# Selective scan: the skip term on ScalarE and in accumulating transfers, the norm's place and four engine orders

## What is computed

```
u, z = x @ Win                               # 512 channels each
uc   = silu(convb + sum_k up[k:k+L] * convw[k])          # 4 taps
x_dbl = uc @ Wx;  B, C from it;  dt = softplus(x_dbl @ Wdt + bdt)
h    = exp(dt * A) * h + (dt * uc) * B       # 32 states, scan over tokens
y    = sum_n h[n] * C[n]  +  uc * Dp         # uc * Dp is the skip term
out  = (y * silu(z)) @ Wout, layernorm, then fusion of both directions
```

## Time and profile before

| | us |
|---|---|
| three runs, median | 4105.2 (4103.2 to 4106.7) |
| profiled execution: time, and span of its core | 4104.3, 4102.7 |
| busy: TensorE, VectorE, ScalarE, GpSimd | 3861.7, 3597.1, 2803.0, 2360.9 |

### The profile page before, as it was taken

How to read it: one execution, slowest core, us unless ns; L and a number is a source line. 1 busy time by engine, 2 the same in 40 slices (tenths; PEclk the granted TensorE clock), 3 DMA queues, 4 the chain that set the end, 5 groups by cost and what they waited for, 6 DMA issues and landing times. The chain is left out here.

```text
span 4102.7 us, 69921 instructions
## 1 busy us (share of the span) xinstructions
PE 3861.7 (94%) x19212; PEld 2880.4 (70%) x19213; DVE 3597.1 (88%) x6830; ACT 2803.0 (68%) x4602; POOL 2360.9 (58%) x2013
## 2 busy tenths in 40 slices
PE   6999999999999999999999969999999699999998
PEld 4666666666666666666666637777777588888887
DVE  7999999999999999999999948998998566666665
ACT  5777777777777777777777847777776345444444
POOL 2555545555455554555655566777777455555555
PEclk8898989898888888888988879999999799999999
DMA  2221222222222212222112222222222455555555
GB/s 73 46 49 35 53 45 51 49 39 49 45 52 47 44 46 43 55 45 50 43 40 55 45 54 78 95 95 91 90 98 80 137 95 94 90 102 95 85 94 86
DMA packets 198462, 272.58 MB, mean 66 GB/s; under 512 B 23377, under 2 KB 143058, under 8 KB 198354
## 3 DMA queue, kind: packets, MB, share of 16 engines
q0 software_dynamic: 94432, 130.60, 17.8%
q1 hardware_dynamic: 100480, 138.48, 12.0%
q10 hardware_dynamic: 3442, 2.21, 0.2%
HBM read 121.07 MB, written 150.14 MB: 66 GB/s over the span
## 5 line engine op out<-in xcount | busy, mean ns | idle before, releaser
L618 PE MATMUL pj<-xt,win 128*128 128x512 f32 x3144 | 934.7, 458 | 49.4 <-DVE xt L793 27.1
L618 PEld LDWEIGHTS pj<-xt,win 128*128 128x128 f32 x3144 | 684.5, 221 | 275.4 <-issue 53.1
L2011 POOL DMA_INDIRECT out<-e_y,e_to x272 | 473.5, 1741 | 365.7 <-ACT e_y L2117 305.3
L806 DVE SCALAR_TENSOR_TENSOR uc<-pj,convw,uc 128x511 f32<-128x511 f32 (+2 forms) x780 | 516.8, 728 | 5.4 <-ACT uc L411 5.4
L326 POOL TENSOR_TENSOR wk<-v,uc 128x512 f32<-128x512 f32 x260 | 347.5, 1336 | 281.2 <-DVE v L854 280.4
L301 POOL TENSOR_TENSOR r<-r,neg_half 128x4 f32<-128x4 f32 x64 | 76.1, 1189 | 667.1 <-ACT r L387 667.1
L666 PE MATMUL po<-yz,wout 128*128 128x512 f32 x1024 | 456.6, 599 | 0.0
L2062 PE MATMUL e_p<-e_w,e_a 128*128 128x256 f32 x3264 | 416.0, 284 | 0.7 <-DVE e_a L2172 0.7
L2062 PEld LDWEIGHTS e_p<-e_w,e_a 128*128 128x128 f32 x3264 | 393.7, 188 | 10.8 <-DVE e_a L2172 1.7
L2050 PE MATMUL e_p<-e_xt,e_w 128*128 128x512 f32 x1632 | 395.5, 398 | 4.5 <-DVE e_xt L2164 2.4
L666 PEld LDWEIGHTS po<-yz,wout 128*128 128x128 f32 x1024 | 189.3, 190 | 262.9 <-issue 262.9
(11 more groups left out here) (243 smaller groups left out, 8806.4 us busy)
## 6 DMA issues: line engine op xcount, KB each, us to landing
e_x<-expert_in SPq DMA_DIRECT2D x138, 260.0 KB, 2.6
bb<-bc SPq DMA_DIRECT2D x65, 512.0 KB, 6.0
h_rows<-fb POOLq DMA_DIRECT2D x64, 512.0 KB, 7.2
h_rows<-h0c SPq DMA_DIRECT2D x32, 512.0 KB, 6.0
a_h<-h_rows SPq DMA_DIRECT2D x128, 128.0 KB
out<-a_bs SPq DMA_DIRECT2D x128, 128.0 KB
bc<-xd SPq DMA_DIRECT2D x65, 128.0 KB, 2.3
e_w1s<-in_moe_w POOLq DMA_DIRECT2D x9, 512.0 KB, 5.2
```

Of the source, the lines that this page charges most:

```text
L618: i = mm(pj[m][:], win[d][wp][:, k, c:c + P], xt[xp][:, k, :], start=(k == 0 and n == 0), stop=(k == KD - 1 and n == 2))
L806: stt(uc[d][:, m, to], pj[m][:, of], convw[d][:, m, tap:tap + 1], uc[d][:, m, to], ALU.mult, ALU.add).then_inc(S["cv"], 1)
L2011: pool.indirect_dma_start(out=out, out_offset=bass.IndirectOffsetOnAxis(ap=to[n][:, j:j + 1].bitcast(U32), axis=0), in_=y[n][:, j, :], in_ ...
```

## The change

- The four skip instructions leave VectorE. ScalarE scales `uc` by `Dp` in place (`skip`), and GpSimd issues two accumulating transfers a slot, from `uc` to `qq` within the on-chip memory (`add_input`); `sums` waits for these (`mix0`, `mix1`). The two instructions that stay in `dead_part` read `wk` (= dt * uc) in place of `v`.
- The norm moves up by one slot: `ln_stats(s+2)` on VectorE behind `gate` of the odd slot, `ln_scale(s+2)` on GpSimd behind `gather(s+2)` of the odd slot, `ln_apply(s+2)` on ScalarE ahead of `decays` of the odd slot.
- GpSimd: all four `wk` first, then all four `tp`, then `add_input`; `row_scale` comes behind `keep_residual` or behind `gather` and `ln_scale`.
- ScalarE: `project_copies` moves into `front`, one part after another, with `skip` between.
- TensorE: `x_dbl` in two halves between the halves of z; `fusion` in two halves, on either side of `dt_proj` (and `turn_x`); `dead_sums` between the halves of the next u; `state_sum` between the halves of `out_proj`.

The diff, cut to its core:

```diff
 # GpSimd
+            def scan_inputs(t, d):
+                pool.wait_ge(S["dt_ok"], t + 1)
+                for m in range(MD):
+                    pool.tensor_tensor(wk[:, m, :], v[:, m, :], uc[d][:, m, :], ALU.mult).then_inc(S["dtu_ok"], 1)
                 pool.wait_ge(S["bcast"], 16 * (t + 1))
+                for m in range(MD):
                     pool.wait_ge(S["dtu_ok"], MD * t + m + 1)
...
                     pool.tensor_tensor(tp[:, m, :], wk[:, m, :], bb[d][:, 0, :], ALU.mult).then_inc(S["tp_ok"], 1)
+            def add_input(t, d):
+                for h in range(NP):
+                    mm = slice(2 * h, 2 * h + 2)
+                    wait_apart(pool, S["q_ok"], NP * t + h + 1)
+                    wait_apart(pool, S["du_ok"], MD * t + 2 * h + 2)
...
+                    pool.dma_start(qq[:, mm, :].rearrange("p m n -> p (m n)"),
+                                   uc[d][:, mm, :].rearrange("p m n -> p (m n)"), accum_op=ALU.add
+                                   ).then_inc(S[f"mix{h}"], 16)
             def slots(s, first):
                 for d in range(DIRS):
                     t = 2 * s + d
-                    if d == 0:
-                        ln_scale(s + 1)
+                    add_input(t, d)
                     if not first:
                         add_rows(t - 2, d, s - 1)
+                    if d == 0:
+                        pool.wait_ge(S["hc_ok"], t + 1)
+                        keep_residual(s + 1)
+                    else:
+                        gather(s + 2)
+                        ln_scale(s + 2)
                     if not (first and d == 0):
                         row_scale(t - 1)
...
+                    scan_inputs(t + 1, 1 - d)
 # ScalarE
+            def skip(t, d, tiles):
+                for m in tiles:
+                    act.wait_ge(S["dtu_ok"], MD * t + m + 1)
+                    act.activation(uc[d][:, m, :], uc[d][:, m, :], ACT.Copy, scale=dp[d][:, m:m + 1]
+                                   ).then_inc(S["du_ok"], 1)
+            def front(t, d, copies):
                 uc_silu(t, d, range(2))
+                if copies:
+                    project_copies(t - 2, range(1))
+                    skip(t - 1, 1 - d, range(2))
                 z_silu(t, d, range(2))
                 uc_silu(t, d, range(2, MD))
+                    skip(t - 1, 1 - d, range(2, MD))
+                if copies:
+                    project_copies(t - 2, range(1, KD))
+                z_silu(t, d, range(2, MD))
                 xd_copy(t, d)
...
+            def back(t, d, s_next=None):
+                last_tap_and_bias(t + 1, 1 - d, range(MD))
                 if s_next is not None:
                     ln_apply(s_next)
...
                 decays(t, d)
 # TensorE
                 in_proj(t, d, 1, range(2))
+                x_dbl(t, d, range(2))
+                in_proj(t, d, 1, range(2, MD))
+                x_dbl(t, d, range(2, MD))
                 if back > 1:
-                    fusion(t - 2, d)
+                    fusion(t - 2, d, (0,))
                 dt_proj(t, d)
                 if turn:
                     turn_x(s_next)
+                if back > 1:
+                    fusion(t - 2, d, (1,))
+                    row_squares(t - 2)
...
+                in_proj(t + 1, 1 - d, 0, range(2))
+                dead_sums(t, d)
+                in_proj(t + 1, 1 - d, 0, range(2, MD))
                 dead_count(t)
+                if back > 0:
+                    out_proj(t - 1, 1 - d, range(1))
                 state_sum(t)
                 if back > 0:
+                    out_proj(t - 1, 1 - d, range(1, KD))
 # VectorE
-                    stt(qq[:, mm, :], over_pair(pss[:]), dall[:], v[:, mm, :], ALU.mult, ALU.mult
+                    dve.wait_ge(S["dtu_ok"], MD * t + 2 * h + 2)
+                    stt(qq[:, mm, :], over_pair(pss[:]), dall[:], wk[:, mm, :], ALU.mult, ALU.mult
                         ).then_inc(S["q_ok"], 1)
-                for m in range(MD):
-                    dve.wait_ge(S["q_ok"], NP * t + m // 2 + 1)
-                    stt(qq[:, m, :], qq[:, m, :], dp[d][:, m:m + 1], uc[d][:, m, :], ALU.add, ALU.mult
-                        ).then_inc(S["q2_ok"], 1)
...
-                    if d == 0:
-                        ln_stats(s + 1)
                     dead_part(t, d)
...
                     gate(t, d)
+                    if d == 1:
+                        ln_stats(s + 2)
```

More of the change, by code:

```diff
@@ L145, in mamba_stage @@
           u_ps a_ok z_ps z_ok uc_ok xd_ps xd_ok bc_ok bcast xd_st dt_ps v_ok vc_ok y_ok l_ok w_ok g_ok
-          d0_ok dt_ok dtu_ok tp_ok da_ok h_ok hc_ok q_ok q2_ok yv_ok yz_ok xm_ok qd_ps gt_ok ct_ok cnt_ps
+          d0_ok dt_ok dtu_ok tp_ok da_ok h_ok hc_ok q_ok du_ok mix0 mix1 yv_ok yz_ok xm_ok qd_ps gt_ok ct_ok cnt_ps
           fl_ok s_ps o_ps fo_ok sq_ok ss_ps rv_ok rr_ok f_ps fin_ok h1_st acc gt2 e_bc e_da e_tp e_h e_hc e_y""".split()
@@ L335, in _ @@
             gather(1)
+            ln_scale(1)
             scan_inputs(0, 0)
@@ L476, in decays, with project_copies @@
                     act.activation(y[:, m, :], v[:, m, :], ACT.Exp, scale=amat[d][:, m, 0:1]).then_inc(S["da_ok"], 1)
-            def project_copies(t):
-                for k in range(KD):
+            def skip(t, d, tiles):
[3 more added lines that the diff above has]
+                                   ).then_inc(S["du_ok"], 1)
+            def project_copies(t, parts):
+                for k in parts:
                     act.wait_ge(S["o_ps"], KD * t + k + 1)
@@ L541, in _ @@
             last_tap_and_bias(0, 0, range(MD))
-            front(0, 0)
+            front(0, 0, False)
             scan_weights()
@@ L549, in _ @@
             softplus_log(0)
-            back(0, 0, False)
+            back(0, 0, 1)
             def slots(s, first):
@@ L554, in slots @@
                     t = 2 * s + d
-                    front(t + 1, 1 - d, s + 1 if d == 0 else None)
+                    front(t + 1, 1 - d, not (first and d == 0))
                     more_states(t, d)
@@ L571, in slots @@
                         finish(t - 1, 1 - d)
-                    back(t + 1, 1 - d, True)
+                    back(t + 1, 1 - d, s + 2 if d == 1 else None)
             slots(0, True)
@@ L576, in _ @@
                 slots(s, False)
+            project_copies(2 * NSEQ - 1, range(KD))
             row_var(2 * NSEQ - 1)
@@ L620, in in_proj, with x_dbl @@
                     i.then_inc(S[ps], 1)
-            def x_dbl(t, d):
+            def x_dbl(t, d, tiles):
                 if not (isinstance(t, int) and t == 0):
                     pe.wait_ge(S["fl_ok"], 3 * t)
-                for m in range(MD):
+                for m in tiles:
                     pe.wait_ge(S["uc_ok"], MD * t + m + 1)
                     i = mm(px[0:NXR, :], wx[d][:, m, :], uc[d][:, m, :], start=(m == 0), stop=(m == MD - 1))
-                i.then_inc(S["xd_ps"], 1)
+                if MD - 1 in tiles:
+                    i.then_inc(S["xd_ps"], 1)
             def dt_proj(t, d):
@@ L658, in state_sum, with out_proj @@
                 mm(pss[:], smask0[:], bcp[:], start=True, stop=True).then_inc(S["s_ps"], 1)
-            def out_proj(t, d):
-                for k in range(KD):
+            def out_proj(t, d, parts):
+                for k in parts:
                     if k == 0 and not (isinstance(t, int) and t == 0):
@@ L679, in row_squares, with fusion @@
                 i.then_inc(S["ss_ps"], 1)
-            def fusion(t, d):
+            def fusion(t, d, halves=range(2)):
                 pe.wait_ge(S["fo_ok"], KD * (t + 1))
                 pe.wait_ge(S["sq_ok"], KD * (t + 1))
-                for h in range(2):
+                for h in halves:
                     for jj in range(2):
@@ L941, in _ @@
             out_weights()
+            ln_stats(1)
             dead_test(0, 0)
```

39 lines of the change are left out of this document (8 added, 31 removed).

## The result

The changed kernel takes 4154.8 us (median of 4 runs, 4153.7 to 4164.5) against 4104.9 us (4103.2 to 4106.7) in the runs of the kernel before beside it: a ratio of 1.0127, with a 95% interval of 1.0109 to 1.0144. The forecast was 4175 us, slower. The profiled execution after took 4153.7 us. One of the four runs of experiment 3 came at a lower granted clock (0.80 against 0.92) and took 4394 us; it is left out of that experiment's time.

The account below looks back on a forecast made before the run. VectorE and TensorE were taken as full. The chain's steps summed to 74.9 us a pair against 72.85, times 32 = +66; with a little of rival A, +70 on 4104.3 us: forecast 4175 us, range 4130 to 4230.

Parts of the forecast that it names:

- step 1: Odd slot, from `dt_ok` through GpSimd's products, transfers and gather issue until the gathers have landed: 26.3 us.
- 6 xt_low to dt_ok: Even slot, from `xt_low` to `dt_ok`, all on VectorE as in the kernel before: 13.4 us.
- rival B: Odd slot: gathers land before `gate` ends, at 23.1 us; pair 71.7 us, time 4068 us; chance 0.15.
- upper bound of 30 us: Odd slot: gathers' landing if three large transfers stand ahead in one queue, each moving data for 4.2 us.
- Step 2: Odd slot, after the gathers: `ln_stats`, `ln_scale`, `row_scale`, `finish` and hand-overs, until `out_proj` can go on: 8.4 us.
- Steps 3 and 4: TensorE from `out_proj` to the dt products, 18.7 us, plus 2.0 us lost to half clock after standing empty 8 us.
- Step 5: From dt products to first v copy 2.2 us, then v copy to `xt_low` 3.9 us: 6.1 us.
- split of 35.8 and 39.1: The predicted pair divided into its odd slot, 35.8 us, and its even slot, 39.1 us.
- Taken at nothing: Work outside the loop, one norm earlier and the last copies later: a few us, counted as zero.
- rival A: TensorE's clock falls a second time, in the even slot; pair 77.6 to 79.3 us, 4257 to 4312 us; chance 0.20.
- D: The transfers come late, so the gathers land at 30 us; pair 78.6 us, time 4289 us; chance 0.08.
- C: Row chain not late, engines' sums decide: VectorE 64.7 or TensorE 66.5 us a pair; time 3902 us; chance 0.12.

Follow-up runs that it names:

- experiment 3: Kernel before with VectorE's four skip instructions left out and nothing in their place: 4067.7 us, 0.9907 of the kernel before.
- experiment 2: Changed kernel with GpSimd issuing the gathers ahead of `add_rows` in the odd slot: 4110.6 us, 1.0012 of the kernel before.
- experiment 4: Changed kernel without the two accumulating on-chip transfers a slot, the skip term left out of the sum: 4108.5 us, 1.0005 of the kernel before.
- experiment 1: Changed kernel with `row_scale` ahead of `ln_scale` on GpSimd in the odd slot: 3972.0 us, 0.9669 of the kernel before.
- experiment 7: Changed kernel with the norm put back in its old place in the even slot: 3917.8 us, 0.9547 of the kernel before.
- experiment 6: Changed kernel with experiment 1 and experiment 2 together, and the prologue's `ln_stats(1)` behind the first softplus: 3943.4 us, 0.9612 of the kernel before.

## Why the prediction was right

The direction held, and so did the path from `ln_stats` on, with `row_scale`, `finish` and `out_proj`. The time at which the gathers land came out by luck (step 1). The chain can be laid beside the changed kernel's rows in the odd slot that begins at 992.66 + 2.27 = 994.93 us. VectorE (start, duration, engine, line, operation; in brackets the idle time ahead and what ended it):

```profile
992.66 2.27 DVE L884 SCALAR_TENSOR_TENSOR v<-v,wk 128x2048 f32<-128x2048 f32 x1
...
1013.54 2.36 DVE L944 TENSOR_TENSOR tp<-tp,qq 128x1024 f32<-128x1024 f32 x2
1015.82 2.35 DVE L953 TENSOR_TENSOR yz<-tp,zs 128x1024 f32<-128x1024 f32 x2
1020.52 1.40 DVE L812 BATCH_NORM_STATS2 stats<-g 128x6 f32<-128x256 f32 x4 [2.35 <-DMA g<-in_table,idc]
...
1048.74 0.68 DVE L844 TENSOR_TENSOR bcp<-px,xd 32x512 f32<-32x512 f32 x1 [3.86 <-ACT xd L441]
...
1054.69 1.29 DVE L823 TENSOR_TENSOR xt<-pj,xt 128x512 fp32r<-128x512 f32 x2 [2.24 <-ACT xt L412]
...
1065.83 2.27 DVE L884 SCALAR_TENSOR_TENSOR v<-v,wk 128x2048 f32<-128x2048 f32 x1
```

GpSimd:

```profile
1004.97 0.87 POOL L340 DMA_DIRECT2D qq<-uc  x1
...
1014.55 1.05 POOL L281 DMA_INDIRECT g<-in_table,idc  x1 [0.30 <-issue]
1022.57 0.20 POOL L289 TENSOR_SCALAR r<-mv 128x4 f32<-128x4 f32 x1 [6.98 <-issue]
...
1026.36 1.00 POOL L301 TENSOR_TENSOR r<-r,neg_half 128x4 f32<-128x4 f32 x1
```

ScalarE:

```profile
1027.54 1.57 ACT L512 ACTIVATE fb<-po,r 128x256 f32<-128x256 f32 x4 [6.48 <-POOL r L301]
...
1050.81 2.42 ACT L450 ACTIVATE v<-pj,bdt 128x512 f32<-128x512 f32 x4 [0.80 <-PE pj L661]
```

TensorE:

```profile
1022.85 0.38 PE L675 MATMUL px<-dgt,ones 128*128 128x4 f32 x2 [1.01 <-DVE dgt L855]
1029.23 5.12 PE L692 MATMUL po<-yz,wout 128*128 128x512 f32 x8 [6.00 <-ACT fb L512]
...
1035.33 3.70 PE L692 MATMUL po<-yz,wout 128*128 128x512 f32 x8
...
1049.65 1.99 PE L661 MATMUL pj<-xd,wdt 16*128 16x512 f32 x8
```

The steps, predicted against read, in this pair and in the mean of the 25 pairs between 300 and 2200 us:

| step | predicted | this pair | mean |
|---|---|---|---|
| 1 gathers landed | 26.3 | 25.6 (to 1020.52) | 25.5 |
| 2 ln_stats to out_proj | 8.4 | 8.7 (to 1029.23) | 8.7 |
| 3, 4 out_proj to dt products, with the clock | 18.7 + 2.0 | 20.4 (to 1049.65) | 21.2 |
| 5 dt products to first v copy | 2.2 | 1.2 (to 1050.81) | 1.2 |
| 5 first v copy to xt_low | 3.9 | 3.9 (to 1054.69) | 3.9 |
| 6 xt_low to dt_ok | 13.4 | 13.4 (to 1068.10) | 13.4 |
| pair | 74.9 | 73.2 | 73.9; of all 32 pairs 74.08 |

**Step 1** came out near by luck: two errors offset each other. The issue was shorter: an on-chip transfer holds GpSimd for 0.87 us, not 1.43, and the last gather's issue ended at 1015.60, 20.7 behind the start, not 25.0. But `ln_stats` could begin only 4.9 us behind that, where the prediction had put 1.3 for the data. With the shorter issue and the 1.3 the gathers would have come at 22.0, ahead of the end of `gate`: that is rival B, 4068 us, and faster. So the direction of the forecast hung on this luck.

That the three transfers ahead in GpSimd's queue add to the 1.3 isn't shown. In the mean of 26 odd slots the last gather's issue ends 21.1 us behind the slot's start in the change and 19.4 in experiments 2 and 4; `ln_stats` begins 4.5 us behind that end in the change, 4.9 in experiment 2 and 4.5 in experiment 4. So the delay is no shorter without the on-chip transfers, or with `add_rows` behind the gathers, and what the two experiments gain (2.06 and 1.47 us a pair) goes with the earlier issue. One cause was left untested: the gathers now share the DMA engines with SyncE's transfers. The queues (packets, MB, share of the engines) around the last gather, before (1013.0 to 1016.0 us), where only GpSimd's queue moves data:

```profile
q0 software_dynamic: 96, 0.26, 29.4%
```

and after (1015.4 to 1020.5 us), where SyncE's hardware queue moves as much as GpSimd's:

```profile
q0 software_dynamic: 315, 0.63, 46.2%
q1 hardware_dynamic: 381, 0.62, 45.8%
```

The transfers' times (line engine operation, count, KB, median us from issue to landing, 300 to 2200 us):

```profile
qq<-uc POOLq DMA_DIRECT2D x104, 512.0 KB, 4.7
h_rows<-fb POOLq DMA_DIRECT2D x52, 512.0 KB, 8.3
...
g<-in_table,idc POOLq DMA_INDIRECT x104, 6.1
```

4.7 us for 512 KB is more than the estimate of 3.2 us that the Trainium skill gives ("DMA: Bandwidth & Descriptors", section "Anatomy of one DMA"); the measurement decides. By that estimate the queue would never hold the gathers; no experiment shows that it sets the landing of the last one. The upper bound of 30 us, with the gathers behind all three transfers, was reached in one slot (30.8); the mean is 25.5.

**Step 2** held nearly to a tenth, and experiment 1 shows that it is the step that decides: with `row_scale` out of this chain 183 us go.

**Steps 3 and 4.** TensorE stands empty for 1.01 us and then for 6.00, 7.0 against the 8 predicted. The first half of `out_proj` takes 5.12 us, the second 3.70: the clock's price here is 1.4 us, not 2.0; in the mean of the pairs both steps take 21.2 us against 20.7 predicted. The clock by stretches (above) is 0.67 in the empty 5.9 us, 0.50 behind it, 1.00 from 1032.20 on. Counted by the clock that the trace lists, before had 53 low stretches that began in 300 to 2200 us, of 451 us together, after 25 of 218 us, one in each pair. So the old low stretches went, as predicted, and a new one came ahead of `out_proj`.

**Step 5** is the one mis-sized term of the other steps. 2.2 us from dt products to the first v copy had been read in a slot of before; here it is 1.16 in every pair. That one us a pair is 32 us, and it with the smaller errors takes the pair from 74.9 to 73.9. The slots' means, 35.45 us odd and 38.63 even, stand beside the split of 35.8 and 39.1. In some odd slots the gathers land 27 to 31 us behind the start of the slot; why wasn't found out.

**Prologue.** "Taken at nothing" was wrong by 7.7 us. The moved norm stands there ahead of the first slot, and VectorE waits for its gather, whose last data land at 63.3 us:

```profile
63.33 1.40 DVE L812 BATCH_NORM_STATS2 stats<-g 128x6 f32<-128x256 f32 x4 [6.10 <-issue]
```

In all, the loop was forecast 30 us too long (70, of which 4 for rival A, against 40) and the prologue and the rest 9 us too short, so 4175 came out 20 us above the result.

**The rivals.** A didn't come: there is one low stretch a pair, none of its own in the even slot. B didn't come either: the gathers land behind the end of `gate`. Experiments 2 and 4 come near its case, with `ln_stats` at 24.3 and 23.9 us, and their pairs of 72.61 and 72.02 come near its 71.7; `ln_scale` and `row_scale` follow in any case. D, the gathers at 30, came in one slot only; `sums` (L944) has no idle time ahead of it, and the transfers land after 4.7 us. C, the engines' sums, was wrong of this change and right of what lies under it: it priced a pair at 66.5 us and the time at 3902, and experiment 7, in which the row chain is short, has 66.95 us and 3917.8. That match is partly luck: C added 4.3 us of clock loss to TensorE's work, and at experiment 7's clock of 0.98 only about 1 us a pair is lost; the rest of its sum wasn't followed. Where the prediction was less clear: it expected VectorE's wait in the even slot at `xt_low` alone; it stands first at `bc_product` (L844, 3.86 us) and then at `xt_low` (2.24).

## What to carry to other kernels

A step that is moved takes its waits to its new place in an in-order queue; look at what is queued behind it there, the smallest and most urgent step above all. Here four tiny instructions on GpSimd cost 183 us by standing ahead of `row_scale`, and the remedy was two lines. Where two engines are full, try the edits that relieve each together (38 and 36 us alone, 186 at once), and move a neighbour's order with an engine's own: TensorE's new order without those of ScalarE and GpSimd cost 144 us.

## What the runs showed of the hardware

- An accumulating transfer of 512 KB from on-chip to on-chip memory held GpSimd for 0.87 us to issue (1.35 for `add_rows`, of the same size, to memory) and landed 4.7 us after issue in the median, against 8.3 for `add_rows`.
- Indirect transfers issued behind such large ones landed 6.1 us after their issue in the median. `ln_stats` began 4.5 us behind the end of the last one's issue, in the mean, with the on-chip transfers ahead and without them (experiment 4). SyncE's transfers moved at the same time (45.8% of the engines around the last gather); what they cost wasn't tested.
- The clock followed TensorE's empty place: 0.67 in the empty 5.9 us, 0.50 in the work just behind, 1.00 from 1032.20 on. This agrees with the Trainium skill, "TensorE: Matmul & The Clock Gate", Part 1 (throttled is the default, activity releases it). An empty place isn't the only thing that lowers it: in the loop of before TensorE was never empty for more than 1.3 us, and the trace lists 53 low stretches. In experiment 6 the mean over the loop was 1.00.
